# Involution block and mixture of experts: per-token products and dense experts replaced by banded matrices and sorted expert tiles

## The reference

```
r    = relu(batchnorm(LN(x) @ w_reduce))                 # 128 -> 32 channels
kgen = r @ w_span + b_span                               # per pixel: 16 groups x 49 taps
conv[b,h,w,g,:] = sum over 49 taps k of kgen[b,h,w,g,k] * LN(x)[b, h+i-3, w+j-3, g, :]   # 8 channels a group
t    = x + conv
p    = softmax(LN(t) @ gate_w + gate_b);  the two largest of 8 are kept as weights we
out  = t + sum over experts e of we[e] * (gelu(LN(t) @ W1[e] + b1[e]) @ W2[e] + b2[e])   # 128 -> 256 -> 128
```

## Time and profile before

| | |
|---|---|
| three runs | 1304.63, 1304.9, 1310.25 us (median 1304.9) |
| span of the profiled execution | 1302.3 us, 27,229 instructions |
| VectorE busy | 1237.1 us, 95% |
| TensorE matmuls busy | 1154.1 us, 89% |
| TensorE weight loads busy | 1081.4 us, 83% |
| GpSimd busy | 1016.6 us, 78% |
| ScalarE busy | 941.2 us, 72% |
| moved by DMA | 28.74 MB, 22 GB/s |

### The profile page before, as it was taken

One profiled execution on the slowest core, in us unless ns is written; L12 is line 12 of the kernel. 1 busy time (PEld: TensorE's weight loads), 2 busy tenths in 40 slices (PEclk: granted clock), 3 DMA queues, 4 the chain that ended last, 5 costly groups with the idle time before them and its releaser, 6 DMA issues. The chain is left out here.

```text
span 1302.3 us, 27229 instructions
## 1 busy us (share of the span) xinstructions
PE 1154.1 (89%) x8857; PEld 1081.4 (83%) x8857; DVE 1237.1 (95%) x1222; ACT 941.2 (72%) x2975; POOL 1016.6 (78%) x558
## 2 busy tenths in 40 slices
PE   3999988999898889989888988898898889998987
PEld 3898888888788878889887888798888878888987
DVE  7789999999999999999999999999999999999942
ACT  3478877776777778777767777787777677667676
POOL 3248888988898898889888988988898889888830
PEclk9899999989999999889999999999999999899999
DMA  4100111011001101100110011011001100000000
GB/s 120 30 22 2 29 30 30 2 28 28 11 18 28 29 0 29 29 25 4 29 28 8 21 28 29 0 29 29 22 7 29 28 8 15 22 15 2 15 8 15
DMA packets 50007, 28.74 MB, mean 22 GB/s; under 512 B 6106, under 2 KB 46906, under 8 KB 49916
## 3 DMA queue, kind: packets, MB, share of 16 engines
q1 hardware_dynamic: 49892, 27.78, 7.8%
q10 hardware_dynamic: 24, 0.00, 0.0%
HBM read 15.38 MB, written 6.42 MB: 17 GB/s over the span
## 5 line engine op out<-in xcount | busy, mean ns | idle before, releaser
L744 DVE TENSOR_TENSOR prod<-kg,xn 112x3584 f32<-112x3584 f32 x224 | 762.0, 3414 | 9.2 <-PE kg L952 7.8
L434 POOL TENSOR_TENSOR prod<-prod 112x1536 f32<-112x1536 f32 x208 | 656.3, 3155 | 144.6 <-DVE prod L744 124.4
L1050 PE MATMUL y<-w_t,hT 128*112 128x128 f32 x3584 | 446.2, 279 | 0.0
L1050 PEld LDWEIGHTS y<-w_t,hT 128*112 128x112 f32 x3584 | 426.6, 184 | 2.1
L621 ACT ACTIVATE weighed<-y,cw 112x128 f32<-112x128 f32 x784 | 224.4, 373 | 140.1 <-DVE cw L837 104.0
L973 PE MATMUL conv<-ident,prod 112*128 112x112 f32 x2472 | 303.0, 276 | 0.0
L973 PEld LDWEIGHTS conv<-ident,prod 112*128 112x128 f32 x2472 | 279.8, 151 | 22.9 <-issue 12.7
L631 ACT ACTIVATE hT<-h,b_t 128x448 f32<-128x448 f32 x448 | 266.9, 657 | 43.0 <-PE h L1039 42.5
L440 POOL TENSOR_TENSOR prod<-prod 112x512 f32<-112x512 f32 (+1 forms) x182 | 249.3, 1370 | 14.3
L764 DVE TENSOR_TENSOR acc<-weighed,acc 112x512 f32<-112x512 f32 x168 | 180.7, 1076 | 18.8 <-ACT weighed L621 18.8
L1037 PE MATMUL h<-tn_hi,w_hi 128*128 128x448 f32 x448 | 182.2, 407 | 16.4 <-ACT hT L631 16.4
(11 more groups left out here) (99 smaller groups left out, 1125.3 us busy)
## 6 DMA issues: line engine op xcount, KB each, us to landing
x_res<-in_x_dram SPq DMA_DIRECT2D x56, 112.0 KB
out_dram<-acc SPq DMA_DIRECT2D x56, 112.0 KB
x_in<-in_x_dram SPq DMA_DIRECT2D x54, 112.0 KB
stage<-xn SPq DMA_DIRECT2D x26, 224.0 KB, 2.7
w_raw<-in_L_ffn_W_dram SPq DMA_DIRECT2D x1, 1024.0 KB, 5.5
w_t<-in_L_ffn_W_dram SPq DMA_DIRECT2D x2, 512.0 KB, 6.3
prod<-in_L_conv_w_span_dram SPq DMA_DIRECT2D x3, 98.0 KB
prod<-in_x_dram SPq DMA_DIRECT2D x2, 112.0 KB
```

What stands on the lines that cost most here:

```text
L434: nc.gpsimd.tensor_tensor(rows[:, :, 0:3 * C], rows[:, :, 0:3 * C], rows[:, :, 3 * C:6 * C], ALU.add).then_inc(fold_step if u in DEEP else ...
L744: nc.vector.tensor_tensor(po, ks, xs, ALU.mult).then_inc(prod_done, 1)
L1050: mm = pe.matmul(y_bank[e % 2][0:T, r * C:(r + 1) * C], hT[e % 2][f][:, r * T:(r + 1) * T], w2_t[:, (2 * e + f) * C:(2 * e + f + 1) * C], ...
```

## The change

Nearly the whole kernel is new. The outer unit is a chunk of 8 image rows of all 4 images (`NC` = 7 chunks, 1,792 tokens each), 16 steps to a chunk (`STEPS` = 4 channel quarters `QUADS` x 4 strips of two rows `STRIPS`). Four steps form a quarter, Q.

- **Normalised image in DRAM.** For each unit of 4 rows (14 of them), `put_xn` writes the normalised rows with 28 DMAs of runs of 256 bytes to a padded, patch-ordered DRAM tensor `xpad`. `load_window` fetches one window for a strip and half of the channels: 112 partitions (14 columns x 8 rows of window positions) x 1792 values, 784 KB; there are 8 to a chunk and five buffers.
- **Kernels as columns of banded matrices.** `kernels(Q, j)`: 4 float32r matmuls with a 98 x 112 slice of `wk` as weights and 112 columns of `rT` as the moving operand, read 8 floats apart; 16 such banks to a quarter. ScalarE (12 of 16) and VectorE (4 of 16) copy each bank to `kb` with a stride of 16 elements in the write, so that a patch's 16 positions lie together.
- **Convolution as matmuls.** `apply(t, pw)`: 4 float32 matmuls, one for each image, weights 112 x 32, moving 112 x 64, each into its own 32 of the 128 output partitions. A step has seven `pw`, 28 matmuls. `take_conv` (VectorE) masks and copies a 128 x 448 bank, `turn_back` transposes it with four matmuls, `add_back` adds it to `t_row`.
- **Sorted experts.** Per chunk a chain of 31 counted VectorE steps finds each token's two experts and its row in a list sorted by expert, padded to tiles of 128 rows. `scatter`: 32 indirect DMAs from GpSimd, 112 rows of 512 bytes each, to `xrows` in DRAM. Then 35 tiles (`NT`): load, transpose, `first_product` (2 float32 matmuls 128 x 128, moving 128), `gelu` on ScalarE (2 x 128 x 128), `second_product` (2 more), bias on VectorE (`put_y`), store to `yrows`. `gather`: 32 indirect DMAs back, `mix`: 32 multiply-adds on VectorE. Before each tile VectorE reads the tile's expert from SBUF into a register and copies that expert's 128 x 642 weights (`stage`).

Experts of a chunk begin 26 steps after its first step, so ten steps, the whole sorted work of the last chunk included, come after the last convolution step. The loops are unrolled. The core of the diff:

```
-            def products(q, bo, u):
-                nc.vector.tensor_tensor(po, ks, xs, ALU.mult).then_inc(prod_done, 1)
-            def folds(q, bo, u):
...
-            def gather_taps(q, bo, u):
...
+            def put_xn(u):
+                sp.wait_ge(xn_ready, u + 1)
+                for half in range(2):
+                    for hh in range(2):
+                        for pw in range(PW):
...
+                            sp.dma_start(to, cols(xs[u % 2], 0, 8)[hh * W + w0:hh * W + w1, :, half * 64:half * 64 + 64]) \
+                                .then_inc(xn_out[u % 2], 16)
+            def scatter(n, i):
...
+                pool.indirect_dma_start(xrows[n % 2], bass.IndirectOffsetOnAxis(ap=pos[n % 2][:, i:i + 1], axis=0),
+                                        tn[:, c * C:(c + 1) * C], None) \
+                    .then_inc(scattered, 16)
+            def stage(n, i):
...
+                at = dve.value_load(te[n % 2][0:1, i:i + 1], min_val=0, max_val=(E - 1) * ROW)
+                dve.tensor_copy(staged[(NT * n + i) % 3][:, :], table[:, bass.ds(at, ROW)]).then_inc(weights_in, 1)
+            def kernels(Q, j):
...
+                for i in range(4):
+                    at = g * IMG + 57 - 8 * (b4 + i) - a
+                    mm = pe.matmul(kg_bank[j % 2][0:WIN, i * PATCHES:(i + 1) * PATCHES], wk[:, at:at + WIN],
+                                   r[:, :, :, b4 + i], start=True, stop=True, skip_group_check=True)
+            def apply(t, pw):
...
+                for b in range(B):
...
+                    to = e_bank[t % 2][32 * b:32 * b + 32, 0:4 * T]
+                    to = to.rearrange("p (g a w c) -> p g a w c", g=4, a=2, c=8)[:, :, :, pw, :]
+                    at = (b * PW + pw) * 64 + (q % 2) * 32
+                    mm = pe.matmul(to, w[:, at:at + 32], rhs, start=True, stop=True, skip_group_check=True)
...
+            for t in range(STEPS * (NC + 3)):
...
+                if live:
+                    apply_wait(t)
+                    for pw in range(PW):
+                        apply(t, pw)
+                        if pw == 1 and more:
+                            kernels(Q + 1, 2 * s)
+                        if pw == 3 and s:
+                            turn_back(t - 1)
+                        if pw == 4 and more:
+                            kernels(Q + 1, 2 * s + 1)
```

More of the change, by code:

```diff
@@ L63, in metaformer_kernel @@
[L63 to L86, removed]
+    assert B == 4 and H == 56 and W == 56 and C == 128 and CR == 32 and HID == 256 and E == 8 and G == 16
@@ new lines, in metaformer_kernel, with slots_at, tiles_out @@
+    PER_STEP = [2, 2, 2, 3]
+    assert sum(PER_STEP) * QUADS == SLOTS
+    def slots_at(t):
+        n, o = divmod(t - STEPS - START, STEPS)
+        if not 0 <= n < NC:
+            return []
+        first = sum(PER_STEP[(START + k) % 4] for k in range(o))
+        return [(n, first + k) for k in range(PER_STEP[(START + o) % 4])]
+    def tiles_out(i):
+        if i % 4 == 3:
+            return [i - 1] if i == SLOTS - 1 else []
+        if i % 4 == 0:
+            return [i - 2, i - 1] if i else []
+        return [i - 1]
@@ L185, in metaformer_kernel @@
[L185 to L188 removed]
+        back = bank("back")
+        xy_bank = bank("xy")
+        h_bank = bank("h")
         pool_const = sem("pool_const")
+        bn_loaded = sem("bn_loaded")
         bn_step = sem("bn_step")
@@ new lines, in turn_back @@
+            def turn_back(t):
+                Q, s = divmod(t, STRIPS)
+                pe.wait_ge(conv_ready, t + 1)
+                if s % 2 == 0 and t >= 2:
+                    pe.wait_ge(t_added, 2 * Q + s // 2)
+                for x_ in range(4):
+                    mm = pe.matmul(back[0:T, s * 128:(s + 1) * 128], conv[t % 2][:, x_ * T:(x_ + 1) * T], ident[:, :],
+                                   is_transpose=True, start=(x_ == 0), stop=(x_ == 3), skip_group_check=True)
+                mm.then_inc(back_done, 1)
@@ new lines, in turn_tn, with gate @@
+            def turn_tn(n, g):
+                k = 4 * n + g
+                pe.wait_ge(tn_ready, 2 * n + g // 2 + 1)
+                misc_free()
+                if k:
+                    pe.wait_ge(tnT_ready, k)
+                for i in range(4):
+                    mm = pe.transpose(misc[:, i * T:(i + 1) * T], tn[:, (4 * g + i) * C:(4 * g + i + 1) * C], row_ident)
+                mm.then_inc(tnt_done, 1)
+            def gate(n, g):
+                k = 4 * n + g
+                pe.wait_ge(tnT_ready, k + 1)
+                for i in range(4):
+                    at = 448 + ((g % 2) * 4 + i) * E
+                    mm = pe.matmul(misc[0:T, at:at + E], tnT[k % 2][:, i * T:(i + 1) * T], gate_sb[:, :],
+                                   start=True, stop=True, skip_group_check=True)
+                mm.then_inc(gate_done, 1)
+                if g % 2:
+                    count["half"] += 1
```

1802 lines of the change are left out of this document (957 added, 845 removed).

## The result

The changed kernel takes **1697.6 us** (median of four runs, 1680.5 to 1711.9) against 1305.1 for the kernel before beside it: ratio 1.296, 95% interval 1.289 to 1.303 (the ratio leaves out the slowest of the four runs, which was in a slower state). It is 30% slower; the forecast was 1332 us with a range of 1130 to 1520. The profiled execution took 1692.9 us, its span is 1691.2.

What follows compares the result with a forecast made beforehand. VectorE was taken to bound the kernel before, with TensorE 10% behind; afterwards SP, TensorE and GpSimd in turn. 90 + 820 + 88 + 114 + 217 = 1329 us of span, forecast 1332 us, range 1130 to 1520.

Steps and rivals of the forecast that it cites:

- the paragraph on TensorE's prices: Unit prices of TensorE's matmuls and transposes, taken from the kernel before, in a stage at granted clock 0.95.
- start: Before the live steps: SP's issues delay the first window to near 60 us and step 2 to about 90 us.
- live steps: The middle, 110 of 112 steps: 1022 us for TensorE's work, its switches and its waits.
- end: After the last convolution step: remaining tiles, routing, scatters, 35 tiles in turn, gathers and stores, 217 us (148 to 309).
- 820 + 114 + 88: Live part: TensorE's work 820 us, eight switches a step to and from `apply` 114, waits 88.
- `apply`: Live part, strip matmuls of the convolution: 28 a step at 0.109 us each, 336 us.
- Rival A: In the live part strips run side by side and changes are free: say 1160 us, faster; chance 0.33.
- A change: Switch between `apply` and full-width work, eight a step: 0.13 us each, 114 us (ends 0 and 229).
- The waits: TensorE's live-part waits: two gelus where tiles follow each other 47 us, last bank and tnT copies 41; together 88.
- B: GpSimd becomes the bound through indirect DMAs at 2.5 us, deciding from about 2.1: 1545 us; chance 0.14.
- C: VectorE stays the bound through register reads: 1600 us at worst at 3 us each, 1450 at 2.4; chance 0.10.
- The sign: Whole kernel against the one before: slower 0.54, faster 0.40, same 0.06; forecast 2% slower.

Runs made afterwards that it cites:

- the grouped run: Changed kernel with a step's seven apply groups issued together, two changes to and from strips instead of eight: 1547.6 us, ratio 1.186.
- experiment 1: Streams of TensorE's work alone, without waits, not the case's computation: mixed step 2.93 us in the changed kernel's order, 2.33 grouped.
- 9: Changed kernel without expert slots, scatters, gathers and mixing: 1114.2 us; the same with each step's strips together: 975.3 us.
- experiment 7: Kernel with strips together: first expert slot moved behind strips, 1522.2 us; also scatters in five steps, 1505.7; also experts two steps later, 1526.8.
- experiment 5: TensorE streams with a ScalarE wait each round, not the case's computation: strips together 3.22 us a round, changed kernel's order 6.51.
- the first kernel with filler: Changed kernel in its own order with three dummy 512-column products before each expert's second product: 1983.1 us, ratio 1.517.
- experiment 6: `wk` and `rT` as fp32 instead of fp32r: with strips together 1839.2 us, ratio 1.410; in the changed kernel's own order 1980.2 to 2023.6 us.

## Why the prediction was wrong

**The step that failed** is the last sentence of the paragraph on TensorE's prices: "The granted clock is 0.95 in the stage these come from." Every price of TensorE was taken over at that clock, for a program that keeps almost nothing of that stage's work; in the live steps the clock was 0.58. None of the three rivals had it either. What the 362 us between 1329 and the span of 1691 are made of:

| part | forecast | measured | where from |
|---|---|---|---|
| start | 90 | 91 | first `apply` at 69.5 (forecast 65), `turn_back` of step 2 at 90.8 |
| live steps | 1022 | 1360 | below |
| end | 217 | 240 | last `apply` ends at 1451 |

That the start agrees is partly luck. The forecast had step 2 begin at 90 us, held by its window; it began near 78, and what stands before 90.8 is a wait of 5.7 us in the middle of step 3, for VectorE's copy behind the load of `t_row`. So the 1360 us hold 108.4 steps and not 110; cut at step 2 as in the forecast, the start is 12 us shorter and the live part 12 longer.

The live steps, against the forecast of 820 + 114 + 88:

- `apply` at the full clock is 0.92 us a step where 3.05 was summed (665.24 to 666.16 in the grouped run, 56 passes): 235 us too much. The four strips do run side by side: a pass takes 0.0164 us, and 64 columns alone would take 0.030 at the fastest pace of the earlier trace rows (448 in 0.21). Rival A was right in this and even too careful, since its half would be 1.53 us a step; the middle between its bound and the others was the wrong choice.
- A change costs 0.10 us at the full clock (experiment 1) and 0.11 at half (9), where 0.13 was taken: 26 us too much at 0.10. It isn't free, as A had it. The Trainium skill's "TensorEngine Tiling (Array Packing)", key properties, calls this a drain; the runs agree that a change costs time and give its price, which the page doesn't.
- By these two corrections the work of TensorE would be 820 - 235 + 88 = 673 us at the forecast's clock. It was busy 1112 us: **439 us are the pace**, by subtraction. A second estimate doesn't use the forecast: with every pair of neighbouring groups at what it takes where this same trace is at 2.4 GHz, the 1112 us would be about 640 (for a tenth of them this trace has no such pair, and 1.75 was taken between the clocks). The two agree within some 30 us, so what is shown is a loss of 440 to 470 us.
- The waits were 250 us and not 88: 162 us more. In the live part alone (90 to 1452 us; the list above is for the whole span) the gelu in front of the second product is 22.1 us and not 47, and the last copy of a quarter and that of tnT are 32.1 + 16.4 and not 41 (each kernel copy 0.93 us and not 0.57). What was missed are the first rows of a chunk (41.1), the bank mask of VectorE in front of `turn_back` (25.9), the gelu in front of a first product (23.5), the transposed rows' copy (23.2), and some 66 us in smaller items.

439 + 162 - 235 - 26 = 340, against 1362 - 1022. The other prices stood: eight kernel matmuls in 0.84 us at the full clock (forecast 0.86), four expert records in 0.47 (0.44), four transposes in 0.49 (0.44). Reading 8 floats apart cost nothing in fp32r, as was said.

**The rivals.** B fell: GpSimd's indirect DMAs are 1.24 us apart, below the 1.47 that was taken and far from B's 2.1.

```profile
1643.40 0.93 POOL L538 DMA_INDIRECT got<-yrows,pos  x1 [44.39 <-DMA yrows<-yo]
1644.63 0.94 POOL L538 DMA_INDIRECT got<-yrows,pos  x1 [0.30 <-issue]
1645.87 0.93 POOL L538 DMA_INDIRECT got<-yrows,pos  x1 [0.30 <-issue]
```

C fell: the register read lies in the 0.25 to 0.76 us before each copy of the weights, and VectorE is busy 34%.

```profile
1567.55 0.50 DVE L905 COPY staged<-table 128x642 f32 x1 [0.55 <-DVE yo L914]
1568.30 0.50 DVE L905 COPY staged<-table 128x642 f32 x1 [0.25 <-issue]
```

A fell by its sign, but half of its mechanism is there: the strips run side by side, and only the changes aren't free. At the full clock the changed kernel in its own order would be about 1250 us by the table's terms (91 + 673 + 250 + 240, with the waits as measured), a little faster than before; the 1074 us of experiment 7 belong to another order. Both are estimates: no run held the full clock.

**The sign** was forecast right (slower, 0.54) by luck: the forecast had 2% from two empty ends around a middle that shrinks from 1234 to 1022 us, and that middle grew to 1360. The range failed on the same step: a middle of 820 us at half pace (90 + 1640 + 114 + 88 + 217) would have given about 2150 us as its upper bound, and was never written down.

**What stays open.** Which property of a stretch of work TensorE's clock follows. Shown is that the same products hold it in one order and lose it in another (5), and that without waits the mix holds it in both (1). But every one of those streams came to its stretch at the full clock, from dense products. The kernel without experts came to its steps at half, and 18 us of the same mix without any wait (623.7 to 641.9 us) did not raise it: whether this mix holds a clock that it can't raise was not tried. The Trainium skill's "TensorE: Matmul & The Clock Gate", Part 1, section on oscillation, has the clock fall where TensorE waits long for a DMA between bursts; here it stayed at half through those 18 us, and held with 0.6 of every 1.98 us spent waiting between dense products. A rule of long waits alone doesn't fit these steps. Not tried either: a convolution with wider moving operands, or kernels built once for two strips.

## What to carry to other kernels

A price of TensorE belongs to a clock, and the clock to the mix of work around it: when a change takes the dense matmuls out, write both clocks' sums before believing either. Put matmuls of one tiling together, here worth 150 us, and the dense ones between the light ones, here worth 25 more; dummy or heavier products to hold the clock cost 286 to 435 us. And read the pace from a known group, not from the printed clock alone.

## What the hardware showed that was not expected

- The clock column prints 1.00 until the first recorded change: up to 123.7 us in the changed kernel, up to 340 us in the first kernel with filler, and for 1068.5 of 1112 us without experts, all at half pace.
- Same products, same wait, other order: 3.22 us a round at 2.4 GHz, 6.51 at 1.2 (experiment 5).
- Short strip passes flow at 0.0155 us, but after 128 of them TensorE stalls 1.5 to 2.3 us in a pure stream (experiment 1): some 14.6 ns for each of the 256 instructions (matmul and weight load). The trace puts the stalls down to issue; that supply is the limit is not shown beyond that. In the kernel the 56 passes of a step run without a stall.
- fp32 columns read 8 floats apart take 0.20 to 0.21 us for a record of 112 columns at either clock (experiment 6), where a dense record of 128 takes 0.11 at the full one; in fp32r the stride can't be seen (0.099 us a matmul with it and without, and the weight loads are busy all the time). The Trainium skill's "SBUF — State Buffer", section on the DMA port swizzle, tells of 16-byte lines that a wider stride leaves at each element; the fp32 runs agree, and one fp32r pass with its 0.05 us of reading has room for it.
- ScalarE's copy from PSUM takes 0.93 us when its writes lie 64 bytes apart, 0.54 in runs; VectorE's 0.91 and 0.62.
